# Splitting the last stage's expert weights once per expert, ahead of time, in a four-layer attention and expert kernel

## What is computed

```python
logits = jnp.einsum('btd,de->bte', x, gate_w)
probs = jax.nn.softmax(logits, axis=-1)
expert_weights, expert_indices = jax.lax.top_k(probs, 2)
expert_weights = expert_weights / expert_weights.sum(-1, keepdims=True)
for i in range(E):
    wi = jnp.where(expert_indices == i, expert_weights, 0.0).sum(-1)
    h = silu(einsum('btd,df->btf', x, w1[i])) * einsum('btd,df->btf', x, w3[i])
    out = out + einsum('btf,fd->btd', h, w2[i]) * wi[..., None]
```

## Time and profile before

| | us |
|---|---|
| median of 3 runs | 1544.19 (1542.02 to 1546.91) |
| the profiled execution | 1546.72 |
| its span on the core | 1545.0 |
| second expert stage, expert 2 to the end | about 444 to 652 |
| block stage, PE's first product to the last landing in ys_dram | 1399.1 to 1529.2 |

### The profile page before, as it was taken

One profiled execution on the slowest core, in us unless ns is written; L12 is line 12 of the kernel. 1 busy time (PEld: TensorE's weight loads), 2 busy tenths in 40 slices (PEclk: granted clock), 3 DMA queues, 4 the chain that ended last, 5 costly groups with the idle time before them and its releaser, 6 DMA issues. The chain is left out here.

```text
span 1545.0 us, 24179 instructions
## 1 busy us (share of the span) xinstructions
PE 1376.5 (89%) x7965; PEld 1174.0 (76%) x7965; DVE 1103.8 (71%) x2259; ACT 944.5 (61%) x1883; POOL 520.8 (34%) x861
## 2 busy tenths in 40 slices
PE   5799899799999999899899999699999999937993
PEld 5688676687888888688778886588878888827993
DVE  3677589887666767867567767577778777736885
ACT  3456777566555555656777777566666666617781
POOL 6315431412121111322312101222344444435883
PEclk7799999999999999999999999899999999968997
DMA  6111242120010001012113100291000000015652
GB/s 165 46 41 36 62 143 78 33 83 1 1 42 21 21 1 41 21 42 63 49 36 123 55 1 1 46 183 18 1 6 10 1 15 1 12 49 168 208 189 92
DMA packets 55995, 85.19 MB, mean 55 GB/s; under 512 B 9400, under 2 KB 37488, under 8 KB 54591
## 3 DMA queue, kind: packets, MB, share of 16 engines
q1 hardware_dynamic: 53375, 79.40, 18.9%
q0 software_dynamic: 2496, 4.24, 0.8%
HBM read 57.90 MB, written 15.78 MB: 48 GB/s over the span
## 5 line engine op out<-in xcount | busy, mean ns | idle before, releaser
L1593 DVE TENSOR_TENSOR hhl<-psum,hhl 128x512 fp32r<-128x512 f32 x336 | 230.3, 687 | 93.0 <-ACT hhl L1098 91.5
L1804 PE MATMUL psum<-xh,wl 128*128 128x512 f32 (+1 forms) x520 | 203.6, 392 | 6.9 <-DVE logits L1313 4.2
L1806 PE MATMUL psum<-xh,wh 128*128 128x512 f32 (+1 forms) x528 | 202.1, 383 | 0.0
L1805 PE MATMUL psum<-xl,wh 128*128 128x512 f32 (+1 forms) x528 | 202.0, 383 | 0.0
L1098 ACT ACTIVATE hhl<-psum 128x512 fp32r<-128x512 f32 x336 | 199.1, 593 | 2.3 <-DVE psum L1589 2.1
L1088 ACT ACTIVATE psum<-psum 128x512 f32<-128x512 f32 x208 | 121.2, 583 | 72.7 <-PE psum L1806 71.9
L904 POOL TENSOR_SCALAR shared<-shared,xrd 128x589 f32<-128x589 f32 x128 | 97.8, 765 | 200.1 <-DVE xrd L1687 199.7
L1170 ACT ACTIVATE hhl<-psum 128x512 fp32r<-128x512 f32 (+1 forms) x160 | 95.4, 596 | 108.1 <-PE psum L2201 105.8
L1589 DVE TENSOR_TENSOR psum<-act_out,psum 128x512 f32<-128x512 f32 x128 | 89.0, 696 | 84.0 <-PE psum L1806 75.0
L1086 ACT ACTIVATE act_out<-psum 128x512 f32<-128x512 f32 x128 | 76.5, 598 | 117.9 <-PE psum L1806 117.5
L2104 PE MATMUL psum<-hhl,wl 128*128 128x512 f32 x336 | 135.3, 403 | 8.2 <-DVE hhl L1593 6.4
(11 more groups left out here) (378 smaller groups left out, 3658.6 us busy)
## 6 DMA issues: line engine op xcount, KB each, us to landing
shared<-in_f_dram SPq DMA_DIRECT2D x16, 768.0 KB
shared<-comb_dram SPq DMA_DIRECT2D x10, 1024.0 KB
xs_dram<-wraw SPq DMA_DIRECT2D x2, 4615.0 KB
shared<-comb_dram SPq DMA_DIRECT2D x24, 256.0 KB, 5.5
wraw<-in_f_dram SPq DMA_DIRECT2D x8, 768.0 KB
xn<-in_f_dram SPq DMA_DIRECT2D x7, 768.0 KB
wraw<-in_f_dram SPq DMA_DIRECT2D x9, 512.0 KB
hhl<-qh SPq DMA_DIRECT2D x64, 64.0 KB, 2.0
```

The source lines that it names most:

```text
L1593: v.tensor_tensor(hl[k % 4], h_bank(f, k), hh[k % 4].bitcast(f32), ALU.subtract).then_inc(f.h_ready, 1)
L1804: mm(dst, ll, rh, start=start, stop=False)
L1805: mm(dst, lh, rl, start=False, stop=False)
L1806: return mm(dst, lh, rh, start=False, stop=stop)
```

## The change

The eight experts' last-stage weights are split once, during F1. SP loads an expert's raw weights (`load_raw`) into one of two halves of `shared`, POOL makes high and low parts in place (`make_parts`: three pairs of a scalar and a subtract instruction on 512 columns), and SP stores the 3072 columns (1.57 MB) to `parts_dram` (`store_parts`). `PARTS_AT` puts experts 0 and 1 behind `split` of expert 2, 2 and 3 behind that of 3, and one behind each of 4 to 7. Attention 2's DVE work waits until all stores have landed. In the block stage each block loads its parts straight into the tiles that PE reads: `up_weights` (2048 columns, 1.05 MB) once PE is done with the up products of block s-3, `down_weights` (1024 columns, 0.52 MB) once it is done with its down products. `up_high`, `down_high`, `up_low` and `down_low` are gone, PE waits for the loads themselves, rows are asked for one block earlier, and POOL runs `send_results(s)` with nothing between. The diff (unchanged lines mostly left out):

```diff
@@ -226,8 +226,10 @@
         xs_dram = nc.dram_tensor("xs_dram", [XROWS, XR], f32, kind="Internal").ap()
+        parts_dram = nc.dram_tensor("parts_dram", [NE, P, 3072], f32, kind="Internal").ap()
+        parts = [shared[:, j * 3072:(j + 1) * 3072] for j in range(2)]
         ys_dram = nc.dram_tensor("ys_dram", [2 * B * S, D], f32, kind="Internal").ap()
-        braw = [shared[:, 3072:4608], shared[:, 4608:6144], yacc[:, 0:1536]]
@@ -288,7 +290,10 @@
         rows_out = sem("rows_out")
-        up_hi, up_lo, dn_hi, dn_lo = sem("up_hi"), sem("up_lo"), sem("dn_hi"), sem("dn_lo")
+        raw_in, parts_made, parts_out = sems("raw_in", 2), sem("parts_made"), sem("parts_out")
+        dn_in = k3_in
@@ -363,6 +368,8 @@
         WIDE_NTH = 3
+        PARTS_AT = {2: (0, 1), 3: (2, 3), 4: (4,), 5: (5,), 6: (6,), 7: (7,)}
@@ -616,6 +623,10 @@
                         spread_routes(f, b)
+                if f is F1:
+                    sp.wait_ge(pt_ready, 2 * NSTEP * 2)
+                    load_raw(0)
+                    load_raw(1)
@@ -623,6 +634,22 @@
                         load_weights(f, e + f.U)
+                    if f is F1:
+                        for j in PARTS_AT[e]:
+                            store_parts(j)
+                            if j + 2 < NE:
+                                load_raw(j + 2)
+            def load_raw(j):
+                if j >= 2:
+                    sp.wait_ge(parts_out, 16 * (j - 1))
+                for a, c, n in ((1024, 0, 1024), (2560, 1024, 512)):
+                    sp.dma_start(parts[j % 2][:, a:a + n], f3[j, :, c:c + n]).then_inc(raw_in[j % 2], 16)
+            def store_parts(j):
+                sp.wait_ge(parts_made, j + 1)
+                sp.dma_start(parts_dram[j, :, :], parts[j % 2]).then_inc(parts_out, 16)
@@ -639,13 +666,22 @@
                     stack_queries(l + 1, 0)
-            def block_weights(s):
+            def expert(s):
+                return sp.value_load(expert_of[0:1, s:s + 1], min_val=0, max_val=NE - 1)
+            def up_weights(s, e):
                 if s >= 3:
-                    sp.wait_ge(up_lo, s - 2)
-                    sp.wait_ge(dn_lo, s - 2)
-                e = sp.value_load(expert_of[0:1, s:s + 1], min_val=0, max_val=NE - 1)
-                sp.dma_start(braw[s % 3], f3[bass.ds(e, 1), :, :].rearrange("e p n -> p (e n)")
+                    sp.wait_ge(b_up, BK * (s - 2))
+                sp.dma_start(bw[s % 3][:, 0:2048].bitcast(f32),
+                             parts_dram[bass.ds(e, 1), :, 0:2048].rearrange("e p n -> p (e n)")
                              ).then_inc(w_in[s % 3], 16)
+            def down_weights(s, e):
+                if s >= 3:
+                    sp.wait_ge(b_down, BK * (s - 2))
+                sp.dma_start(bw[s % 3][:, 2048:3072].bitcast(f32),
+                             parts_dram[bass.ds(e, 1), :, 2048:3072].rearrange("e p n -> p (e n)")
+                             ).then_inc(dn_in[s % 3], 16)
@@ -664,14 +700,24 @@
             for s in range(3):
-                block_weights(s)
+                e = expert(s)
+                up_weights(s, e)
+                down_weights(s, e)
...
                 block_rows(s, first[s])
-            for s in range(3, NBLK):
-                block_rows(s, first_row(s))
-                block_weights(s)
+            for s in range(3, NBLK + 1):
+                if s == 3:
+                    block_rows(3, first_row(3))
+                    block_rows(4, first_row(4))
+                elif s + 1 < NBLK:
+                    block_rows(s + 1, first_row(s + 1))
+                if s < NBLK:
+                    up_weights(s, expert(s))
+                if s > 3:
+                    down_weights(s - 1, expert(s - 1))
@@ -814,6 +860,15 @@
                 ins.then_inc(f.split, 1)
+            def make_parts(j):
+                pool.wait_ge(raw_in[j % 2], 16 * 2 * (j // 2 + 1))
+                w = parts[j % 2]
+                for h, lw, n in ((0, 1024, 512), (512, 1536, 512), (2048, 2560, 512)):
+                    hi, lo = w[:, h:h + n].bitcast(f32r), w[:, lw:lw + n]
+                    st.link(g.tensor_scalar(hi, lo, 1.0, 1.0, ALU.mult, ALU.mult))
+                    ins = g.tensor_tensor(out=lo.bitcast(f32r), in0=lo, in1=hi.bitcast(f32), op=ALU.subtract)
+                ins.then_inc(parts_made, 1)
@@ -853,6 +908,9 @@
                     split(f, e)
+                    if f is F1:
+                        for j in PARTS_AT[e]:
+                            make_parts(j)
@@ -915,11 +973,6 @@
                 send_rows(TB * 3 + i // 2, i % 2)
-            def up_low(s):
-                pool.wait_ge(up_hi, s + 1)
-                g.tensor_tensor(out=bup[s % 3][1], in0=braw[s % 3][:, 0:1024],
-                                in1=bup[s % 3][0].bitcast(f32), op=ALU.subtract).then_inc(up_lo, 1)
@@ -928,13 +981,8 @@
                                          bounds_check=2 * B * S - 1, oob_is_err=False).then_inc(results_out[s % 3], 16)
-            up_low(0)
-            up_low(1)
-            for s in range(NBLK + 4):
-                if s + 2 < NBLK:
-                    up_low(s + 2)
-                if s >= 4:
-                    send_results(s - 4)
+            for s in range(NBLK):
+                send_results(s)
@@ -1197,20 +1245,6 @@
             route_exp(F3, 3)
-            def up_high(s):
-                act.wait_ge(w_in[s % 3], 16 * (weight_loads[s % 3] + s // 3 + 1))
-                if s >= 3:
-                    act.wait_ge(b_up, BK * (s - 2))
-                else:
-                    act.wait_ge(xo_ready, 5 * NU)
-                a.activation(bup[s % 3][0], braw[s % 3][:, 0:1024], ACT.Copy).then_inc(up_hi, 1)
-            def down_high(s):
-                act.wait_ge(w_in[s % 3], 16 * (weight_loads[s % 3] + s // 3 + 1))
-                if s >= 3:
-                    act.wait_ge(b_down, BK * (s - 2))
-                a.activation(bdn[s % 3][0], braw[s % 3][:, 1024:1536], ACT.Copy).then_inc(dn_hi, 1)
@@ -1237,9 +1271,6 @@
                 a.activation(yT[s % 2], bank(SUM_BANK, BS), ACT.Copy).then_inc(b_yT, 1)
-            up_high(0)
-            down_high(0)
-            up_high(1)
@@ -1250,12 +1281,8 @@
                     high(k - 1)
-                if k % 2 == 0 and s + 2 < NBLK:
-                    up_high(s + 2)
...
                     block_high(s + 2)
-                if k % 2 and s + 1 < NBLK:
-                    down_high(s + 1)
@@ -1507,6 +1534,8 @@
                     dve.wait_ge(cols_ps, 1)
+                elif l == 2:
+                    dve.wait_ge(parts_out, 16 * NE)
@@ -1737,11 +1766,6 @@
             give_shares(3)
-            def down_low(s):
-                dve.wait_ge(dn_hi, s + 1)
-                v.tensor_tensor(bdn[s % 3][1], braw[s % 3][:, 1024:1536], bdn[s % 3][0].bitcast(f32),
-                                ALU.subtract).then_inc(dn_lo, 1)
@@ -1768,7 +1792,6 @@
                 v.tensor_copy(ys[s % 3].rearrange("p h c -> p (h c)"), bank(BACK_BANK, BS)).then_inc(yr_done, 1)
-            down_low(0)
@@ -1779,8 +1802,6 @@
                     block_low(s + 2)
-                if k % 2 and s + 1 < NBLK:
-                    down_low(s + 1)
@@ -2263,7 +2284,7 @@
                 if c == 0:
-                    pe.wait_ge(up_lo, s + 1)
+                    pe.wait_ge(w_in[s % 3], 16 * (weight_loads[s % 3] + s // 3 + 1))
@@ -2283,7 +2304,7 @@
                 if c == 0:
-                    pe.wait_ge(dn_lo, s + 1)
+                    pe.wait_ge(dn_in[s % 3], 16 * (2 * NG + NG + s // 3 + 1))
```

## The result

The changed kernel takes 1539.2 us (median of 15 runs, 1534.92 to 1542.12). The kernel before, in runs beside it, takes 1544.94 us (15 runs, 1540.17 to 1548.98). The ratio is 0.9963, with a 95% interval of 0.9952 to 0.9975: 0.37% or 5.7 us faster. The prediction was 1540.0 us and 4.2 us faster. The profiled execution took 1540.04 us with a span of 1538.3 us, 6.7 us less than the span before.

A forecast was written before the change was run, and what follows sets the result against it. PE was taken to bound the kernel, busy 89% of 1545.0 us. Stalls gone (-8.2 us) plus a later start (+4.0) gave -4.2 us, 1540.0 us against the 1544.19 us median; range 1537 to 1543, 8 in 10 1536.5 to 1547.0.

The forecast's parts named there:

- the three outcomes: Whole kernel against a 0.3% mark: faster by more 0.40, the same 0.48, slower 0.12.
- The steady blocks: Blocks 4 to 22: PE's period falls from 5.12 to 4.70 us per block, a gain of 7.5 us.
- Its cause: Block stage: up_high's 0.94 us wait and 1.06 us run on ACT hold `result`, so block_down idles 0.42 us per block.
- The stalls in blocks 0 to 4: Before block 4: one stall of 0.65 us at 1413.13 goes, bringing the gain to 8.2 us.
- The later start: Block stage start: 2.36 MB more queue ahead of block 0's rows, costing 4.0 us (2.5 to 6.5).
- The rival that the send lands only when the weights have drained: Block stage start: rows issued near 1400, landing at 1402.5 or more; 6 us later, net -2.2; chance 0.18.
- DMA: the term: Block stage: DMA needs 4.85 us per block, 0.15 above PE's; 2.9 of 5 us load lead used, cost 0.
- the lower bound: Block stage: least DMA work per block, weights 3.85, rows 0.33 and two sends 0.40 us, 4.57 us.
- the DMA rival: Block stage: DMA becomes the bound; net -1.6 at 5.10 us per block, +7.0 at 5.55; chance 0.22, half of it slower.
- The hidden work: Second expert stage: 47 us of POOL splitting and 18.9 MB of traffic hide behind PE, cost 0; at most 5.9 us once.
- After the last block: Behind block 22: last sends, their landing and the loads of ys_dram follow as before; nothing changes.

The follow-up runs named there:

- e1: The kernel before, plus the changed kernel's parts made and stored in the second expert stage, which nobody reads; block stage untouched: 1544.62 us, ratio 1.0006.
- e4: The changed kernel with ACT's two removed conversions put back on unused data, waiting for no load: 1539.46 us, ratio 0.9947.
- e10: The kernel before, but from block 3 on each weight load brings 512 of 1536 columns, all conversions kept: 1535.9 us, ratio 0.9944.
- ctl_after: The changed kernel, unchanged, timed a second time beside the runs that reorder SyncE's first loads: 1538.57 us.
- e5: The changed kernel with POOL's removed subtraction put back on unused data and the sends four blocks late as before: 1542.74 us, ratio 0.9973.
- e6: The changed kernel with 0.26 MB more loaded per block from the fourth on, into an unused buffer: 1545.58 us, one run.
- e7: The changed kernel with 0.52 MB more loaded per block from the fourth on: 1558.14 us, one run.
- e11: The changed kernel with SyncE's first loads in order of use, only block 0's up weights ahead of the rows: 1533.46 us, ratio 0.9913.
- e9: The changed kernel with only block 0's up weights ahead of three blocks' rows, then up 1, down 0, up 2, down 1, down 2: 1536.86 us.
- e2: The changed kernel with only block 0's weights ahead of the rows, the others behind the rows block by block: 1537.01 us, ratio 0.9949.
- e8: The changed kernel with block 0's weights first, then the rows of blocks 0 to 2, then the weights of blocks 1 and 2: 1537.84 us.
- e3: The changed kernel with two blocks' weights (3.1 MB) ahead of the rows instead of three: 1536.18 us, ratio 0.9949.

## Why the prediction was right, and where it was not

The time (1540.0 against 1539.2 us) and the range held, and the mechanism was the one forecast. That the times agree to 0.8 us is in part luck: the change was 1.5 us larger than forecast, and the median of the kernel before was 0.75 us above the one that the forecast started from. Of the three outcomes I gave most, 0.48, to a change within 0.3%; it came out at 0.37%, with an interval (0.25 to 0.48%) that lies across that mark. The two profiles differ by 6.7 us where the sum said 4.2. Over all profiles with the same code in a stage the terms are 3.1 us for the start, 1.0 us less in blocks 1 to 3 and 7.8 us less in blocks 4 to 22, which makes 5.7 us, as the medians do.

**The steady blocks: right.** The forecast was 4.70 us per block and 7.5 us over 18 blocks; they take 4.68 us and gave 7.95 us (7.64 us against e1).

**Its cause: right in place, half right in kind.** The text named ACT's wait of 0.94 us and its 1.06 us of work together as what stood ahead of `result`. e4 and e10 part them: the wait made most of the stall (5.95 of 7.95 us), and the work alone makes none. So, as I read it, a load that lands about 1 us earlier should have given the kernel before most of this gain without any splitting in advance; that was not tried with whole loads.

**The stalls in blocks 0 to 4: mis-sized.** The forecast took the one stall of 0.65 us at 1413.13; the four blocks gave 1.19 us. Block 0 itself is no good measure, since PE's granted clock rises from 0.50 near 1406 both in the changed kernel and in ctl_after, though their first products start at 1402.74 and 1401.51: it took 4.67 us in the changed kernel and 5.39 us in ctl_after, which is the same code. Blocks 1 to 3 took 13.74 us in both, 14.81 us before and 14.66 us in e1: 0.9 to 1.1 us. I had read one idle row and not compared the length of these blocks with each other.

**The later start: right, and in its parts too.** The forecast was 4.0 us (2.5 to 6.5); the first product came 3.61 us later, 3.1 us by the means over nine profiles. The text let the weights end near 1399.6 and the rows land near 1400.9. DMA stayed full until 1400 and the rows landed at 1400.48. Of the 0.43 MB that DMA moved from 1399 to 1401, 0.40 MB are the rows of three blocks, so by my estimate the weights were out shortly after 1399. The send itself took longer as well, which the text did not have (6.62 instead of 4.87 us), but it landed at 1396.52, 4 us ahead of the rows. It does not set the start: in ctl_after it took 0.73 us less than in the changed kernel and the start came only 0.25 us sooner, in e5 0.88 us less and the start 0.43 us later. The rival that the send lands only when the weights have drained did not occur, since DMA was still full behind it (0.96 of the time from 1396 to 1399). The prediction calls this its third rival where it cites the rule; it is the second in its list.

**DMA: the term was too high, the conclusion right.** I took 4.85 us per block and let it use up 2.9 of 5 us of slack. e6 and e7 put it at 4.5 us, below PE's 4.68 us, so no slack was used; the lower bound, 4.57 us, was the better one. With the added 0.26 MB the block takes 5.1 us and the DMA rival's mechanism is there as described: in e6 it eats nearly all of the gain (one run of 1545.58 us, beside 1546.37 us for the kernel before). The Trainium skill's 358 GB/s from HBM to SBUF ("DMA: Bandwidth & Descriptors", section "Where 436 GB/s comes from") would have bound the block at 4.39 us for weights alone plus the rest; the trace shows 384 GB/s over 80 us, and e6 and e7 402 to 405 GB/s when DMA is the bound. With one core at work the measurement decides: the 358 GB/s did not bind.

**The hidden work: right in cost, wrong in one reading.** Cost 0, shown by e1 within 0.23%. But the text had POOL idle for 27.96 us before each `split` and 16 us of cover left. Before the second `split` of the stage it was idle for only 11.23 us, and the change put two experts' parts, 11.8 us, just there. That PE did not wait was luck as far as the text goes: it rests on the time between this `split` and PE's use of it, which the text did not work out for this gap.

**After the last block: right, though these two profiles differ.** "Nothing changes" seems to leave out 1.17 us. The last eight sends of results follow each other every 1.28 us, and the program ends behind them. POOL of the kernel before at the start of this row of sends, then of the changed kernel, then of e1, whose block stage is that of the kernel before:

```profile
1518.15 0.97 POOL L926 DMA_INDIRECT ys_dram<-shared,wraw  x1 [1.90 <-issue]
```

```profile
1511.61 0.98 POOL L979 DMA_INDIRECT ys_dram<-shared,wraw  x1 [2.20 <-DVE shared L1793]
```

```profile
1514.02 0.97 POOL L962 DMA_INDIRECT ys_dram<-shared,wraw  x1 [1.58 <-DVE shared L1807]
```

That is 7.29 us after block 22's start in the first, and 6.28 us in both others. From block 22's start to the end, e1 takes 32.86 us, less than the changed kernel's 32.97 us, and ctl_after takes 33.08 us. So the extra 1.0 us is one profile's and not the old code's. A part of it is a stall before block_down that e1 does not have there:

```profile
1515.04 0.36 PE L2294 MATMUL psum<-hhl,ab 128*128 128x256 f32 x1 [0.40 <-issue]
```

**The side that I did not see** is what the start could have given. The forecast treated "weights ahead of the rows" as a price of the change. It is a price of its order of issue: e11 takes back 5.6 us of A to first product, more than the change had cost, and its way from block 0 to block 22 is as long as the changed kernel's (102.93 us, against 102.59 and 103.31 us in the changed kernel and ctl_after).

## What to carry to other kernels

Before an engine's work is taken away because it sits in front of a stall, look at whether it works or waits there; a wait for a load goes with an earlier or smaller load. Transfers in one queue belong in the order of their use, the small ones above all: moving one late transfer forward only shows the next one, so write out the order for every transfer up to the steady state. And when a stage moves twice the bytes, price what is queued behind the first loads, not only the rate of the steady state.

## What the runs showed of the hardware

**One core's DMA ceiling here is 402 to 405 GB/s over 60 to 80 us** (e6 and e7, one run each; 427 GB/s were seen over 2 to 3 us) in mixed loads of 1 MB, 0.5 MB and 0.13 MB with GpSimd's sends among them, and the share of time is 1.02 just below it (384 GB/s) and 1.03 at it. At 384 GB/s PE still has work for 80.00 of 80 us.

**A GpSimd send of rows is slowed by another queue's loads.** From its start to its landing it took 2.42 and 2.53 us with 1.05 MB issued ahead (e9, e11; in e9 DMA had gone quiet, 0.20 of the time from 1387 to 1388), 3.76 and 3.94 us with 1.57 MB (e2, e8), 4.87 to 5.00 us with 2.36 MB (before, e1, e10), 5.96 us with 3.15 MB (e3) and 5.74 to 6.62 us with 4.72 MB (the six profiles above). From 3.15 MB on no growth shows beyond that spread. With the most bytes ahead it does not wait for their end: it landed at 1396.52 in the changed kernel, some 4 us before DMA went quiet.

**A pause costs PE more than its length.** In e9, PE's clock was full before the 4.20 us pause and fell to half of it behind (the clock is the last but two of the columns):

```profile
1399.00:1403.00 4.00, 0.48 (x5) 0.27 (x3) 2.23 (x6) 0.89 (x2) 0.00 (x0) 1.00 1.06 398
1404.00:1407.00 3.00, 3.00 (x16) 3.00 (x15) 0.07 (x1) 1.36 (x3) 0.00 (x0) 0.50 0.29 99
1408.00:1411.00 3.00, 3.00 (x27) 3.00 (x27) 2.07 (x6) 1.62 (x4) 0.00 (x0) 1.00 0.91 325
```

The block with the pause took 9.69 us: 4.62 us as in the other kernels, 4.20 us of pause, and 0.9 us behind it, where the clock stood at 0.50 and products took 0.41 us each instead of 0.28 us. Two more kernels agree. In e8 a pause of 2.99 us was followed by a clock of 0.50 from 1410 to 1413, in e5 one of 3.09 us by 0.50 from 1414 to 1417; the block with the pause and the next one took 3.85 and 3.97 us more than the usual 4.62 and 4.49 us together, so 0.9 us beyond the pause in each. In e2 the pause of 1.89 us fell into block 0, ahead of the clock's rise: the clock was still at 0.56 of full speed from 1402 to 1405, and the block took 7.78 us, so 5.89 us without the pause, where block 0 takes 4.51 to 5.70 us in the other kernels. So no clear price of a pause shows there.
